# Second and third attention of an eight-layer chain: scores computed twice, probabilities formed already transposed in PSUM

## The reference

```
x = x + tanh(g_xattn[n]) * attn_n(layernorm(x), ctx, ctx)      n = 0..3
x = x + tanh(g_ffn[n])   * ffn_n(layernorm(x))
```

```
score = einsum('bhqd,bhkd->bhqk', qh, kh) / sqrt(dh)
attn  = softmax(score);  out = einsum('bhqk,bhkd->bhqd', attn, vh);  return out @ wo.T + bo
```

## Time and profile before

| | |
|---|---|
| median of three executions | 3624.97 us |
| the profiled execution | 3616.34 us, span 3614.6 us |
| busy share of the span | PE 71%, DVE 59%, POOL 44%, ACT 41% |
| l1, from the first to the last row maximum | 1007.9 to 1394.4 us |
| l2, the same | 1754.6 to 2307.2 us |
| l3, from the first to the last L721 | 2735.4 to 3294.1 us |
| mean granted TensorE clock | 0.791 |

### The profile page before, as it was taken

The page is one execution under the profiler, slowest core; times in us unless marked ns, Lnnn a source line. Parts: engine busy times, 40 slices in busy tenths (PEclk is TensorE's granted clock), DMA queues, the critical chain, the costliest instruction groups (busy, mean ns, idle before and its releaser), DMA issues. The chain is left out here.

```text
span 3614.6 us, 84054 instructions
## 1 busy us (share of the span) xinstructions
PE 2554.5 (71%) x30961; PEld 1981.4 (55%) x30971; DVE 2132.0 (59%) x4394; ACT 1498.5 (41%) x2492; POOL 1596.1 (44%) x2184
## 2 busy tenths in 40 slices
PE   5999999977678886233687766609956877665490
PEld 4878778764557775122465555506634665554260
DVE  3767777661166664676578788854424666677312
ACT  3555555532255553677343333202215665553120
POOL 1333433440164430775024666440017788884207
PEclk9999999988888887555688778659976766675795
DMA  4000000003300000000000000015531000000243
GB/s 143 17 18 22 23 21 21 20 8 112 99 26 22 22 19 13 1 1 1 26 10 12 23 22 23 20 61 153 161 106 32 23 25 27 27 23 13 79 128 93
DMA packets 192979, 153.50 MB, mean 42 GB/s; under 512 B 24426, under 2 KB 170461, under 8 KB 192582
## 3 DMA queue, kind: packets, MB, share of 16 engines
q1 hardware_dynamic: 176198, 116.45, 11.0%
q0 software_dynamic: 16384, 31.69, 2.9%
HBM read 97.54 MB, written 52.43 MB: 41 GB/s over the span
## 5 line engine op out<-in xcount | busy, mean ns | idle before, releaser
L979 PE MATMUL l_B<-l_val,l_prob_t 128*64 128x18 f32 x6144 | 348.6, 220 | 44.1 <-ACT l_prob_t L822 36.9
L979 PEld LDWEIGHTS l_B<-l_val,l_prob_t 128*64 128x64 f32 x6144 | 340.4, 149 | 59.3 <-issue 59.3
L903 PE MATMUL l_PT<-const_table,l_prob 128*128 128x128 f32 x1536 | 267.9, 332 | 38.0 <-ACT l_prob_t L822 28.6
L1971 PE MATMUL experts_H<-experts_xs_t,experts_w 128*128 128x512 f32 x576 | 272.1, 616 | 10.1 <-ACT experts_hid L1951 4.9
L903 PEld LDWEIGHTS l_PT<-const_table,l_prob 128*128 128x128 f32 x1536 | 237.3, 178 | 68.8 <-issue 58.0
L822 ACT COPY l_prob_t<-l_PT 128x512 f32<-128x512 f32 x384 | 209.6, 601 | 132.8 <-PE l_PT L903 132.7
L203 POOL DMA_INDIRECT l_got<-rows,l_index x192 | 220.2, 1147 | 94.7 <-POOL l_index L196 50.3
L358 POOL TENSOR_TENSOR l_products<-l_router_w,xn_all 128x1024 f32<-128x1024 f32 x100 | 236.3, 2390 | 32.3 <-DVE logits L464 32.0
L883 PE MATMUL l_A<-const_table,l_xn 128*128 128x128 f32 x192 | 59.6, 410 | 251.7 <-issue 139.1
L328 POOL DMA_INDIRECT slots<-xn_all,put x192 | 202.0, 1052 | 60.6 <-issue 49.5
L632 POOL TENSOR_TENSOR l_var_eps<-l_mv,eps 128x2 f32<-128x2 f32 x96 | 26.4, 275 | 430.4 <-DVE l_mv L775 430.3
(11 more groups left out here) (309 smaller groups left out, 6835.8 us busy)
## 6 DMA issues: line engine op xcount, KB each, us to landing
experts_w<-in_F_w SPq DMA_DIRECT2D x104, 256.0 KB, 2.9
experts_xs<-slots SPq DMA_DIRECT2D x72, 256.0 KB, 2.8
rows<-experts_y SPq DMA_DIRECT2D x72, 256.0 KB, 2.9
l_ctx_t<-in_ctx_t SPq DMA_DIRECT2D x96, 128.0 KB, 2.1
slots<-l_zeros SPq DMA_DIRECT2D x64, 96.0 KB
experts_w<-in_F_w SPq DMA_DIRECT2D x40, 128.0 KB, 2.5
slots<-l_zeros SPq DMA_DIRECT2D x8, 512.0 KB, 5.5
l_ctx_t<-in_ctx_t SPq DMA_DIRECT2D x64, 64.0 KB, 2.0
```

Source lines behind the costliest of these rows:

```text
L903: last = nc.tensor.transpose(PT[:, c % 2, P * a:P * a + P], prob[:, t.par(5), c, a // 2, 2 * (a % 2):2 * (a % 2) + 2, :].rearrange("p j k ...
L979: last = nc.tensor.matmul(B[64 * b:64 * b + 64, col:col + 18], prob_t[:, 4 * (hp // 2) + 2 * tile + hp % 2, 64 * b:64 * b + 64], val[:, t. ...
L1971: nc.tensor.matmul(H[:, c, :], w1_s[:, t.par(2), c, :], xs_t[:, t.par(2), :], start=True, stop=True).then_inc(h_filled[c], 1)
```

## The change

l1 and l2 are made by a new function, `attention_split`; l3 keeps `attention_narrow`. In the new function:

- The scores are computed twice. `X` has queries on partitions, as before, and only its row maxima are used. `Z` has keys on partitions; the exponential of it is P in the layout that the product with the values wants. The transposes of P and their copies are gone.
- The maxima must be subtracted from `Z`, where they run along the free axis. DVE splits each into three bfloat16 parts, PE transposes them with one matmul (`TOP`), DVE spreads them into `top_d`, and PE adds them to `Z` with a matmul by -1.
- For the mask, PE adds `hide` (0 or -2^100 in bfloat16) by an identity matmul into `X` and into `Z`.
- The zeroed versions of k and q (`k_m`, `q_m`) are no longer written by ScalarE. Two tensors are zeroed once and SP copies eight partitions at a time from `k_t` and `q_t` into them, with 16 DMAs each.
- The router of l2 becomes a `Router`: logits by matmul instead of products on GpSimd and sums on DVE.
- In all phases, `Head` and `Router` use row numbers and rows where they lie instead of copying them first (the loops of GpSimd are written out).

```
 def gather(self, nc, pool, t, s, ready, count):
-        for k in range(self.ks):
-            last = nc.gpsimd.tensor_copy(self.index[:, t.par(s), k, :], g.get[k][:, bass.ds(t.item(s) * 2, 2)])
-        last.then_inc(self.index_done, 1)
...
-                wait(pool, self.index_done, n0)
-                wait(pool, self.terms_done, n2)
+                wait(pool, self.terms_done, t.done(s + 2))
                 pool.indirect_dma_start(self.got[:, t.par(s), k, tile, :], None, self.rows,
...
+def attention_split(nc, g, name, gate_col, wq, bq, wk, bk, wv, bv, wo, bo, kind, mask=None, head=None, router=None):
+    STAT, NORM, TURN, PROJ, SCORE, PROB, OUT, STREAM = range(1, 9)
...
+        def _(sp):
...
+            def step(t):
+                if t.live(2):
+                    wait(sp, xv_filled, beats(t.t - 2, TURN, XV_BEATS) if t.t >= 8 else 0)
+                    sp.dma_start(ctx_t[:, t.par(2, 6), :], g.ctx_t[:, t.item(2) * 256:t.item(2) * 256 + 256]).then_inc(ctx_in[t.par(2, 6)], 16)
+                if t.live(PROJ):
+                    slot = t.par(PROJ, 3)
+                    if not stable:
+                        wait(sp, qk_drained, t.done(PROJ))
+                        wait(sp, s_filled, t.done(PROJ + 3))
+                        for row in range(0, P, 8):
+                            sp.dma_start(k_m[row:row + 8, slot, row // 8 % 4, :], k_t[row:row + 8, slot, :]).then_inc(k_masked[slot], 16)
+                    wait(sp, qk_drained, t.done(PROJ))
+                    wait(sp, p_filled, t.done(PROJ + 3))
+                    for row in range(0, P, 8):
+                        sp.dma_start(q_m[row:row + 8, slot, row // 8 % 4, :], q_t[row:row + 8, slot, :]).then_inc(q_masked[slot], 16)
...
+        def _(dve):
...
+                    wait(dve, s_filled, n5)
+                    V.tensor_reduce(top[:, :, :].rearrange("p r a -> p (r a)"), X[:, :, :].rearrange("p r (a k) -> p (r a) k", k=64),
+                                    AX.X, ALU.max).then_inc(top_done, 1)
...
+                    V.tensor_copy(split[:, :, 0, :], top[:, :, :]).then_inc(hi_done, 1)
...
+                    wait(dve, top_filled, n5)
+                    wait(dve, p_filled, t.done(SCORE + 2))
+                    V.tensor_tensor(top_d[:, t.par(SCORE), :, :], TOP.unsqueeze(1).broadcast_to([P, 8, P]),
+                                    g.const[:, C_AMASK:C_AMASK + 8].unsqueeze(2).broadcast_to([P, 8, P]), ALU.mult).then_inc(diag_done, 1)
...
+        def _(act):
...
+                            nc.scalar.activation(prob_t[:, t.par(PROB), r, :], Z[:, r, :], ACT.Exp).then_inc(prob_done, 1)
...
+                    nc.scalar.activation(k_t[:, t.par(PROJ, 3), :], QK[:, 256:512], ACT.Identity, bias=bk_s[:, :])
+                    nc.scalar.activation(q_t[:, t.par(PROJ, 3), :], QK[:, 0:256], ACT.Identity, bias=bq_scaled[:, :],
+                                         scale=SCALE).then_inc(qk_drained, 1)
...
+        def _(pe):
...
+                if t.live(PROB):
+                    wait(pe, q_masked[slot], 16 * reused(t, PROB, 3))
+                        wait(pe, diag_done, n6)
...
+                                    nc.tensor.matmul(Z[64 * b:64 * b + 64, r, 256 * tile:256 * tile + 256], minus_ones[rows, :],
+                                                     top_d[rows, t.par(PROB), 4 * tile:4 * tile + 4, 64 * b:64 * b + 64],
+                                                     start=tile == 0, stop=False)
...
+                                last = nc.tensor.matmul(Z[64 * b:64 * b + 64, r, 256 * tile:256 * tile + 256], k_t[rows, slot, seq],
+                                                        q_m[rows, slot, :, seq], start=stable and tile == 0, stop=tile == 1 and not folded)
...
+                if t.live(SCORE) and not stable:
+                    wait(pe, k_masked[slot], 16 * reused(t, SCORE, 3))
+                    wait(pe, diag_done, n6)
...
+                                last = nc.tensor.matmul(X[64 * b:64 * b + 64, r, 256 * tile:256 * tile + 256], q_t[rows, slot, seq],
+                                                        k_m[rows, slot, :, seq], start=not folded and tile == 0, stop=tile == 1)
...
+                    last.then_inc(s_filled, 1)
+                if t.live(PROJ):
...
+                    nc.tensor.matmul(QK[:, 0:256], wq_s[:, :], xn_t[:, t.par(PROJ), :], start=True, stop=True).then_inc(qk_filled, 1)
...
+                                    last = nc.tensor.matmul(Z[side:side + 64, 2 + b, 9 * h:9 * h + 9], term[rows, t.par(OUT), h // 4, col:col + 64],
+                                                            val[rows, t.par(OUT), tile, h, :],
+                                                            start=k == 0, stop=k == len(terms) - 1)
...
-        attention_narrow(nc, g, "l1", 1, t["L1_wq"], t["L1_bq"], t["L1_wk"], t["L1_bk"], t["L1_wv"], t["L1_bv"],
+        attention_split(nc, g, "l1", 1, t["L1_wq"], t["L1_bq"], t["L1_wk"], t["L1_bk"], t["L1_wv"], t["L1_bv"],
```

More of the change, by code:

```diff
@@ L52, in constants @@
     c[:, C_BLK:C_BLK + 16] = np.arange(16) * SLOTS
-    c[:, C_ITEM:] = np.arange(TOP2_TILES)
+    c[:, C_ITEM:C_AMASK] = np.arange(TOP2_TILES)
+    for a in range(8):
+        c[:, C_AMASK + a] = np.arange(P) % 8 == a
     return c
@@ L210, in combine @@
-        landed = t.landed(s, 2 * self.ks)
-        tiles = bass.ds(t.item(s) * 2, 2)
+        g, par, n = self.g, t.par(s), t.done(s)
+        tiles = slice(t.item(s) * 2, t.item(s) * 2 + 2)
         xs = g.x[:, tiles, :]
+        others = (self.got[:, par, 0, :, :], g.xn[:, tiles, :] if self.own else self.got[:, par, 1, :, :])
         pool.wait_ge(ready, count)
[L214 to L219, removed]
@@ L220, in combine @@
-        if self.own:
-            last = nc.gpsimd.tensor_tensor(self.term[:, 1, :, :], g.xn[:, tiles, :],
-                                           g.weight[1][:, tiles].unsqueeze(2).broadcast_to([P, 2, D]), ALU.mult)
+        wait(pool, self.arrived[par], t.landed(s, 2 * self.ks))
+        wait(pool, self.combined, t.done(s + 1))
+        for k in range(2):
+            last = nc.gpsimd.tensor_tensor(self.term[:, k, :, :], others[k], g.weight[k][:, tiles].unsqueeze(2).broadcast_to([P, 2, D]),
+                                           ALU.mult)
@@ L1141, in transpose @@
         for tile in range(self.tiles):
-            last = nc.tensor.transpose(out[:, P * tile:P * tile + P], self.xn_s[:, t.par(s + 2), tile, :], self.g.const[:, C_IDENT:C_IDENT + P])
+            last = nc.tensor.transpose(out[:, P * tile:P * tile + P], self.g.xn[:, t.item(s + 2) * self.tiles + tile, :], self.g.const[:, C_IDENT:C_IDENT + P])
         return last
@@ L1196, in dve @@
             dve.wait_ge(self.w_in, self.loads)
-            wait(dve, updated, n_updated)
+            wait(dve, read, n_read)
             if self.kind == "top2":
@@ L2361, in lay_out @@
          "g_xattn": a["g_xattn"], "g_ffn": a["g_ffn"], "consts": constants()}
[L2363 removed]
+    m = a["mask_BxSxS2_bf1"].view(np.uint8)
+    o["mask"] = np.stack([x.reshape(TILES, P, SEQ).transpose(1, 0, 2) for x in (m, m.transpose(0, 2, 1))])
     def halves(w):
```

503 lines of the change are left out of this document (444 added, 59 removed).

## The result

| | before | after |
|---|---|---|
| median of the executions beside each other | 3626.9 us (4) | 4056.09 us (4; 4052.58 to 4060.8) |
| ratio | | 1.1185, 95% interval 1.1165 to 1.1204 |
| span of the profiled execution | 3614.6 us | 4054.9 us |

The change makes the kernel 11.9% slower. The forecast was 3554 us; the result lies 346 us above the upper end of the range.

The account below looks back on a forecast made before the run. Before, l1 was near PE's limit, l2 DVE's, l3 GpSimd's; after, SP's issues bound l1 and nearly l2. l1 +50, l2 -97, l3 -24: -71 on 3616.3, 3545; plus 8.6 for the median, 3554 us; range 3449 to 3710.

Parts of the forecast that it names:

- SP's pitch: Start-to-start time of SP's small copies in l1 and l2: between 0.38 and 0.63 us, taken as 0.41.
- 33 pitches + 0.3: SP's time an item in l1 and l2: 33 issues plus 0.3 us for four waits, 13.8 us.
- Case C: SP's list in l1 and l2: issue pitch 0.46 us or more, slower; at 0.50, +90 us, 3715; chance 0.33.
- break-even of 0.456: SP's issue pitch in us at which the total passes the time before, with SP bounding l1 and l2.
- ring of k: Loop of projection, k copies, landing and scores in l1 and l2: 12.2 us an item, hidden under SP's 13.8.
- Case B: Cheaper issues hide SP in l1 and l2; rings decide, 11.5 and 13.5 us an item; 3449 us, chance 0.15.
- PE and DVE: Engine work an item in l1 and l2: PE about even, under 13 us; DVE about 10.3 us in l2.
- Case D: PE's granted clock falls to 0.65 or below in l1 and l2: -2 us, no change; chance 0.07.
- Edges: Phase starts and ends: l1's first X +9 us, l2's start +15, l2's end -12.
- Head in l3: GpSimd's row-number copy in l3: about 0.86 us an item goes, for about 28 of 32 items, -24 us.

Follow-up runs that it names:

- e7: e2's kernel plus, in l1, sixteen probe copies an item into an unread scratch tensor, from HBM or SBUF, 8 or 128 partitions; 3393.88 us.
- e4: The changed kernel with its 32 copies an item taking 4 partitions each instead of 8, output not the reference's; 3934.17 us.
- e5: The changed kernel without its 16 copies of q an item, second scores reading a zero q_m; 3744.47 us.
- e1: The changed kernel with weight columns permuted, so four strided copies of 32 partitions replace sixteen for each of k and q; 3442.66 us, ratio to before 0.9513.
- e2: The changed kernel with ScalarE writing k_m and q_m by eight activations and SP's copies taken out; 3385.74 us, ratio to before 0.9352.
- e9: The kernel before with only Head changed, row numbers read where they lie without GpSimd's copy; 3614.93 us against 3623.93, ratio 0.9972.
- e10: e2's kernel unchanged, run again in another job on another chip; 3567.89 us, ratio to before 0.9847.
- e3: The changed kernel with its 32 copies an item taking 16 partitions each instead of 8, output not the reference's; 4040.82 us.
- e6: e1's kernel with each of the eight copies an item moving all 128 partitions, output not the reference's; 3455.64 us.

## Why the prediction was wrong, point by point

**SP's pitch: the step that failed.** "I take 0.41" was sized from the router load behind a short transfer, a load from HBM, and the bound above it (0.63) from loads from HBM to 64 partitions. All rows used had HBM as source; the copies go from SBUF to SBUF, which the trace before never does. Measured 0.668, outside both ends. e7 shows that size carried over rightly (0.30 for 8 partitions from HBM) and that the pair of memories did not. The reading behind 0.41, "behind a short transfer the next issue is quicker", doesn't hold in the trace before either. `l_bk` there stands directly behind the 0.5 KB of `l_bq` and takes 0.43:

```profile
1727.28 0.43 SPq L584 DMA_DIRECT2D l_bk<-in_L_bk  x1
```

The prediction named the unknown as "no row has eight partitions" and missed the other half of it.

**The form of the sum was right.** 33 pitches + 0.3 with 0.668 gives 22.3 us an item; measured 22.24 and 22.38. Case C as written gives, with this pitch, l1 31 x (22.34 - 12.47) + 9 = +315, l2 31 x (22.34 - 17.83) + 3 = +143, l3 -24: +434, so 4059 us, and the median is 4056.09. The case with a chance of 0.33 came true, with a pitch beyond the 0.58 that it was priced to. e4 is a second point on this line: its pitch of 0.617 gives 20.7 us an item and 3955 us, and its one execution took 3934.17. The break-even of 0.456 was not reached by any run with 32 copies an item.

**The rings.** The ring of k was 12.2 us with 6.6 for the issues; 10.65 in their place gives 16.2, and e5 measured 17.15 in l1. Taken by itself it hid under SP, as said. Case B's "rings decide", 11.5 and 13.5 us, 3449 in total, is about what remains once SP is relieved: e1 has 11.02 and 14.77 and 3442.66, e2 10.36 and 13.53 and 3385.74. That e1's total is so near is luck in part: l1 came out below and l2 above.

**PE and DVE.** Prices from PE's order of time in l2 in e2, at the higher clock:

```profile
1799.78 1.12 PE L1648 MATMUL l_X<-l_k_m,l_q_t 32*64 32x256 f32 x32
...
1802.96 2.05 PE L1696 MATMUL l_Z<-l_val,l_prob_t 64*64 64x9 f32 x128
...
1809.07 0.63 PE L1608 MATMUL l_Z<-l_top_d,l_minus_ones 32*64 32x256 bf16 x16 [0.85 <-issue]
...
1810.50 1.05 PE L1622 MATMUL l_Z<-l_hide,const_bf 128*128 128x256 bf16 x8
```

Scores as predicted (1.12), values product 2.05 (predicted 2.5), the matmul by -1 0.63 (below 1.12), the mask 1.05 for each of two (2.1, the lower end). DVE in l2 was put at 10.3 us an item: in e2 it is 67% of 13.53 = 9.1.

**Case D.** PE's granted clock did fall in l1, to 0.59. It is a result here, not the cause: SP's list is full whatever PE's clock, and in e1 and e2 nearly the same work on PE has 0.78 and 0.84 again.

**Edges.** The first X of l1 came 2.5 us later (predicted 9). l2 from SP's first issue to the first maximum took 43.1 us instead of 29.1 (+14, predicted +15). The end of l2, from the last maximum to the next phase's first issue, took 108.5 instead of 108.8 (predicted -12). Why the missing products saved nothing there is not shown. In e2, with SP out of the way, the next phase begins 101.8 us behind the last maximum.

**Head in l3.** Right in sign, too large: -24 predicted, -12.9 in the changed kernel's trace, -9.8 in e9, where it was changed alone. GpSimd was costed as full in every item, at 84 busy of 100, and its whole gap was counted; by the rows e9 saves 0.97 us of it an item and an item gets 0.32 shorter, so something else bounds most items. What that is, no run here shows.

**The Trainium skill's** rule against many transfers to disjoint partitions ("DMA: Bandwidth & Descriptors", section "Rules for kernel authors") gave the right side, but for another reason than its own. The rule speaks of transfers to two halves of the partitions, which share the same 16 DMA engines. Here these engines were 10 to 13% busy in l1 and l2, and what stood one behind the other was SP's issues. A quarter of the issues brought 613 us (e1).

## What to carry to other kernels

Before work is moved to DMAs, count the issues an item and price one from a row with the same source and destination memory, not only the same size; where no such row exists, a probe of some copies in a queue that is free settles it in one run. When two phases of different arithmetic show the same time per item and no engine is busy, look at the list of the DMA queue: in this trace a full one showed up mostly as waits that end with "issue". A layout that lets one strided copy do the work of four, or eight more activations on a ScalarE that has room, made the same idea about 5 to 6.5% faster than the kernel before instead of 12% slower (1.5% in the one job told under e10).

## What the runs showed of the hardware

- An issue on SP takes, in the median, 0.58 us (4 partitions, e4), 0.62 (8, the changed kernel; 0.68 in e7), 0.59 (16, e3), 0.60 (32, e1, and 128, e6) for copies of 1 KB a partition from SBUF to SBUF; from HBM to SBUF 0.30 (8 partitions) and 0.43 (128), both in e7; from SBUF to HBM 0.33 to 0.46 (96 to 256 KB, e2).
- The program of e2, with PE at 90% in l1, was 5.4% slower in one of three jobs, each on its own chip (e10), with pauses of some 0.45 us inside runs of 16 ns matmuls (2.05 us for 128), while the kernel before took the same there as elsewhere.
